# Two small loads move to ScalarE's queue, three more warming products, and one bias product moves behind the first weights of tile 0

## The chip, the cores and the metric

The kernel runs on one core of one Trainium2 chip. Its time is device microseconds (us), the median of several runs; beside them one execution was profiled, and its trace is what the rows below come from. TensorE (PE) does the matrix products, VectorE (DVE) and ScalarE (ACT) the elementwise work, SyncE (SP) issues the transfers (DMAs) between device memory and the on-chip memory; GpSimd (POOL) has almost nothing to do.

## What is computed

An audio tower on 64 x 7 = 448 rows. Patches of 1024 numbers are normalised, scaled by g1 and shifted by b1, multiplied by a 1024 x 512 matrix, given a bias, and normalised again (g2, b2). Then come attention with 16 heads of width 128 and an 8-bit-rounded feed-forward product, both added to the stream. The change touches the first step alone:

```python
def _L0_tok_ref(x, W, b, g1, b1, g2, b2):
    x = x[:, :n_patch * TIN, :].reshape(bsz, n_patch, TIN * F)
    x = layer_norm(x, g1, b1, EPS)
    x = jnp.einsum('bpd,dh->bph', x, W) + b
    return layer_norm(x, g2, b2, EPS)
...
h = _L0_tok_ref(x, L0_tok_W, L0_tok_b, L0_tok_g1, L0_tok_b1, L0_tok_g2, L0_tok_b2)
h = h + _L0_attn_ref(_layernorm(h, axis=-1), L0_attn_W_Q, L0_attn_W_K, L0_attn_W_V, L0_attn_W_O)
h = h + _L0_ffn_ref(_layernorm(h, axis=-1), L0_ffn_weight, L0_ffn_weight_scale, L0_ffn_bias)
```

## The kernel before

The 448 rows are four tiles of 112 rows. Each engine has its own program, written out by hand in order; engines meet only at semaphores, and an engine that waits holds back all that stands behind it in its program.

**SyncE** issues every load, all on one queue. The first are the two halves of patch tile 0 (`x_in`), then, once VectorE has cleared two tiles, the bias row `tok_b`, the identity `ident_sb` for transposes, and the two columns `g1_col` and `b1_col` (the trace calls them g_col and b_col; 128 partitions of 8 numbers, so many tiny pieces). Behind them come the embedding weights `tokw_raw` in four pieces of 512 KB with patch tile 1 between the first and the second, then patch tiles 2 and 3, the rows g2 and b2, the mask, and the heads' weights.

**TensorE** first runs `keep_warm`: WARM_START = 6 small products of a tile of ones with itself, whose result nobody reads. Then it waits for `tok_b` to land and starts the accumulators of tiles 1, 2 and 3 with their bias (`begin_with_bias`, line 342: a product of a tile whose first row is ones with a tile whose first row is the bias, 112 x 512). Then `patch_transposes(0)` (line 336) turns the normalised tile 0 in eight pieces; `begin_with_bias(0)`; and `embed(0)` (line 353) multiplies the eight turned pieces by the eight slices of weights, two slices for each landed piece of weights. A matrix product in full 32-bit precision shows as two records in the trace. Before slice 6 of `embed(0)` stand the transposes of tile 1, before slice 4 of `embed(1)` those of tile 2, and so on; from there on the program goes through the tiles, then through the heads in pairs, then through the feed-forward part.

**ScalarE** takes the square root for tile 0's norm (line 686; its first root loads the table of the function), normalises the second half of tile 0 (line 691), waits for the two columns, and then copies the turned pieces out of PSUM in eight instructions (line 702, `patch_evacuate`), in which it applies g1 and b1. `take_root` waits for all twelve constants `eps_4`.

**VectorE** clears tiles and writes constants, then takes tile 0's mean and variance (lines 949, 951), makes the reciprocal root in four small steps (lines 960 to 983) and normalises the first half of tile 0 (line 1063). For tiles 1 and 2 it does the same up to line 983 and ScalarE normalises the whole tile.

Of the kernel before, what the change touches and what calls it, by code (L numbers as in the profile page):

```python
# [7 lines left out]
ACT = mybir.ActivationFunctionType  # L8
# [7 lines left out]
ROWS = BATCH * PATCHES  # L16
IN_DIM = 1024
D = 512
WARM_START, WARM_STATS, WARM_RSTD, WARM_SCALE = 6, 2, 3, 3
HEADS, E = 16, 128  # L20
PAIRS = HEADS // 2
TILES = 4
KD_ALL, KD_HALF = D // 128, D // 256
TR = ROWS // TILES
KIN = IN_DIM // 128
# [14 lines left out]
ROOTS = {0: LN_EPS, 1: LN_EPS, 2: LN_EPS, 3: LN_EPS, TILES: LN_EPS, 2 * TILES: NORM_EPS, TILES + 1: LN_EPS,  # L40
         2 * TILES + 1: NORM_EPS, TILES + 2: LN_EPS, 2 * TILES + 2: NORM_EPS, TILES + 3: LN_EPS,
         2 * TILES + 3: NORM_EPS}
# [6 lines left out]
def audio_tower(nc, patches, tok_w, heads_w, ffn_w, tok_g1, tok_b1, tok_b, tok_g2, tok_b2,  # L49
# [4 lines left out]
    with ExitStack() as ctx:  # L54
        def sb(name, shape, dt=F32):
            return ctx.enter_context(nc.sbuf_tensor(name, shape, dt))

        def sem(name):
            return ctx.enter_context(nc.semaphore(name))
# [4 lines left out]
        g1_col = sb("g1_col", [128, KIN])  # L64
        b1_col = sb("b1_col", [128, KIN])
# [59 lines left out]
        eps_4 = sb("eps_4", [TR, len(ROOTS)])  # L125
        root = sb("root", [TR, len(ROOTS)])
        last_root = sb("last_root", [TR, TILES])
# [15 lines left out]
        cols_landed = sem("cols_landed")  # L143
# [5 lines left out]
        x_landed = [sem(f"x_landed{t}") for t in range(TILES)]  # L149
# [8 lines left out]
        eps_ok = sem("eps_ok")  # L158
# [72 lines left out]
        def loop_pairs(eng, step):  # L231

            with eng.Fori(0, (PAIRS - 2) // 2) as i:
                step(i * 4 + 2, i * 2 + 1, 1)
                step(i * 4 + 4, i * 2 + 2, 0)
# [5 lines left out]
        @block.sync  # L241
        def _(sp):
            def load(dst, src, landed):
                sp.dma_start(dst, src).then_inc(landed, 16)

            def load_tokw(i):
                a, b = TOKW_PIECES[i]
                load(tokw_raw[:, a:b, :], tok_w[:, a:b, :], tokw_landed[i])

            for c, landed in ((slice(0, 512), x_landed[0]), (slice(512, IN_DIM), x0_rest_landed)):  # L250
                load(x_in[:, 0, c], patches[0][:, c], landed)
            sp.wait_ge(bias_cleared, 2)
            load(tok_b_rows[0:1, :], tok_b[0:1, :], tok_b_landed)
            load(ident_sb[:], ident, ident_landed)
            load(g1_col[:], tok_g1, cols_landed)
            load(b1_col[:], tok_b1, cols_landed)
            load_tokw(0)
            load(x_in[:, 1, :], patches[1], x_landed[1])
            load_tokw(1)
            load_tokw(2)  # L260
            load_tokw(3)
            load(x_in[:, 2, :], patches[2], x_landed[2])
            load(x_in[:, 3, :], patches[3], x_landed[3])
            load(g2_row[:], tok_g2.to_broadcast([TR, D]), rows_landed)
            load(b2_row[:], tok_b2.to_broadcast([TR, D]), rows_landed)
            load(mask_sb[:], mask, late_landed)
            load(ffn_scale_col[:], ffn_scale.to_broadcast([128, 1]), late_landed)
            sp.wait_ge(ffn_b_cleared, 1)
            for row in (0, B_LO):
                load(ffn_b_raw[row:row + 1, :], ffn_bias, late_landed)  # L270
            def load_qkv(h, s):
                sp.dma_start(raw_qkv[s][:], heads_w[h][:, 0:QKV]).then_inc(qkv_landed[s], 16)

            def load_out(h, s):
                sp.dma_start(raw_out[s][:], heads_w[h][:, QKV:WCOLS]).then_inc(out_landed[s], 16)

            for s in range(2):
                load_qkv(s, s)
            for s in range(2):
                load_out(s, s)  # L280
            sp.dma_start(ffnw_raw[:], ffn_w).then_inc(ffnw_landed, 16)
            for s in range(2):
                sp.wait_ge(qkvw_hi_ok, s + 1)
                sp.wait_ge(qkvw_lo_ok, s + 1)
                load_qkv(s + 2, s)

            def load_pair(a, p, g):
                for s in range(2):
                    sp.wait_ge(qkvw_hi_ok, a + (s + 1))
                    sp.wait_ge(qkvw_lo_ok, a + (s + 1))  # L290
                    load_qkv(a + (s + 2), s)
                for s in range(2):
                    sp.wait_ge(outw_hi_ok, a + (s - 1))
                    sp.wait_ge(outw_lo_ok, a + (s - 1))
                    load_out(a + s, s)

            loop_pairs(sp, load_pair)
            for s in range(2):
                sp.wait_ge(outw_hi_ok, HEADS - 3 + s)
                sp.wait_ge(outw_lo_ok, HEADS - 3 + s)  # L300
                load_out(HEADS - 2 + s, s)
            for i, (t, c) in enumerate(RESULTS):
                sp.wait_ge(y_ok, i + 1)
                sp.dma_start(out[t][:, c], h_sb[:, t, c]).then_inc(out_stored, 16)
            sp.wait_ge(out_stored, 16 * len(RESULTS))
# [3 lines left out]
        def _(pe):  # L309
# [14 lines left out]
            def patch_transposes(t):  # L324
                if t == 0:
                    pe.wait_ge(ident_landed, 16)
                    pe.wait_ge(x0_half_normed, 1)
                else:
                    pe.wait_ge(x_normed, t + 1)
                if t >= 2:  # L330
                    pe.wait_ge(xt_ok, KIN * (t - 1))
                for k in range(KIN):
                    if t == 0 and k == KIN // 2:
                        pe.wait_ge(x_normed, 1)
                    b = 2 * (t % 2) + k // 4
                    mm = nc.tensor.transpose(bank[b][:, k % 4 * TR:(k % 4 + 1) * TR],  # L336
                                             x_in[:, t, k * 128:(k + 1) * 128], ident_sb[0:TR, 0:TR])
                    if k % 4 == 3:
                        mm.then_inc(xt_ps, 1)

            def begin_with_bias(t):
                nc.tensor.matmul(acc[t][0:TR, :], first_ones[:], tok_b_rows[:], start=True, stop=False,  # L342
                                 skip_group_check=True)

            def embed(t, ahead_of):
                for k in range(KIN):
                    if k in ahead_of:
                        ahead_of[k]()
                    for i, (first_chunk, _) in enumerate(TOKW_PIECES):
                        if t == 0 and k == first_chunk:  # L350
                            pe.wait_ge(tokw_landed[i], 16)
                    pe.wait_ge(xt_ok, KIN * t + k + 1)
                    last = nc.tensor.matmul(acc[t][0:TR, :], xt[:, t % 2, k * TR:(k + 1) * TR], tokw_raw[:, k, :],  # L353
                                            start=False, stop=(k == KIN - 1), skip_group_check=True)
                last.then_inc(tok_ps, 1)
# [31 lines left out]
            keep_warm(WARM_START, acc[TILES - 1])  # L387
            pe.wait_ge(bias_ones_ok, 1)
            pe.wait_ge(tok_b_landed, 16)
            for t in range(1, TILES):  # L390
                begin_with_bias(t)
            patch_transposes(0)
            begin_with_bias(0)
            embed(0, {KIN - 2: lambda: patch_transposes(1)})
            embed(1, {KIN // 2: lambda: patch_transposes(2)})
            embed(2, {KIN // 2: lambda: patch_transposes(3)})
            stream_transposes(0)
# [280 lines left out]
        def _(act):  # L678
            def hi_part(dst, src):
                return nc.scalar.copy(dst, src)  # L680

            def take_root(c):
                i = list(ROOTS).index(c)
                act.wait_ge(variance_ok, i + 1)
                act.wait_ge(eps_ok, len(ROOTS))
                nc.scalar.activation(root[:, i:i + 1], moments[:, c, 1:2], ACT.Sqrt, bias=eps_4[:, i:i + 1],
                                     scale=4.0).then_inc(root_ok, 1)
# [38 lines left out]
            def split_out(p, s):  # L726
                act.wait_ge(out_landed[s], (p + 1) * 16)
                hi_part(outw_hi[s][:], raw_out[s][:]).then_inc(outw_hi_ok, 1)

            take_root(0)  # L730
            normalise(0, slice(IN_DIM // 2, IN_DIM))
            act.wait_ge(cols_landed, 32)
# [192 lines left out]
        def _(dve):  # L925
# [127 lines left out]
            nc.vector.memset(tok_b_rows[:], 0.0).then_inc(bias_cleared, 1)  # L1053
            dve.wait_ge(bias_cleared, 1)
            nc.vector.memset(first_ones[0:1, :], 1.0).then_inc(bias_ones_ok, 1)
            nc.vector.memset(ffn_b_raw[:], 0.0).then_inc(ffn_b_cleared, 1)
            nc.vector.memset(ones_r[:].bitcast(F32), 1.0).then_inc(ones_ok, 1)
            for i, eps in enumerate(ROOTS.values()):
                nc.vector.memset(eps_4[:, i:i + 1], 4.0 * eps).then_inc(eps_ok, 1)
            patch_moments(0)  # L1060
            need(rsqrt_from_roots([0]))
            negative_mean_scaled(0).then_inc(x_scaled, 1)
# [237 lines left out]
```

## Time and profile before

| | us |
|---|---|
| three runs | 265.77, 266.09, 267.23 (median 266.09) |
| the profiled execution, its own time | 266.61 |
| its span, first to last instruction | 264.8 |
| TensorE busy in the span | 256.3 (97%) |
| share of TensorE in the chain that ended last | 91% |

A span is 1.8 us shorter than the execution's own time. Times in the rows are microseconds from the span's start. SPq rows are the issuing of a transfer, not the transfer. PEld is the loading of stationary data, which overlaps the product before it. The time between two starts is TensorE's pace; a record's own length is longer than that, since products overlap.

### The profile page before, as it was taken

The numbers are of one execution on the slowest core, as the hardware profiler recorded it, in microseconds if no ns is written. First come the engines' busy times: TensorE is split into PE (matmuls) and PEld (weight loads), VectorE is DVE, ScalarE is ACT, GpSimd is POOL, SyncE is SP. The second block draws the span as 40 slices with busy tenths as digits, with TensorE's granted clock in tenths as the row PEclk, the third lists the DMA queues.
The fourth block names the chain that finished last, engine by engine and source line by source line (L and its number), as shares of the span: only waits on it lengthen the run. The fifth ranks groups of instructions, "written<-read, shape, count | busy, mean of one in ns | idle before, by whom it ended". The sixth has DMA issues, their size and how long they took to land.

```text
span 264.8 us, 3840 instructions
## 1 busy us (share of the span) xinstructions
PE 256.3 (97%) x1422; PEld 218.0 (82%) x1422; DVE 157.7 (60%) x321; ACT 124.8 (47%) x216; POOL 0.2 (0%) x4
## 2 busy tenths in 40 slices
PE   7999999999899999999999999999999999999984
PEld 5444447898799999999999999999999999998662
DVE  6257977825828913962493269038723968934884
ACT  2567864444714543533361445425343642536680
POOL 0000000000000000000000000000000000000000
PEclk9999999999999999999999999999999999999999
DMA  5999030141080053032306210630230020000004
GB/s 163 346 272 398 6 119 0 26 155 59 9 308 2 15 186 119 1 110 88 119 0 198 76 43 0 198 119 0 62 136 0 2 79 0 2 0 0 0 4 139
DMA packets 7585, 23.57 MB, mean 89 GB/s; under 512 B 1251, under 2 KB 1715, under 8 KB 7446
## 3 DMA queue, kind: packets, MB, share of 16 engines
q1 hardware_dynamic: 7574, 23.42, 27.2%
q8 instruction: 7, 0.11, 0.2%
q14 instruction: 4, 0.03, 0.0%
HBM read 22.50 MB, written 0.92 MB: 88 GB/s over the span
## 4 chain that ended last, share of the span: by engine, by line
PE 91%; DVE 5%; DMA 1%; issue 1%; ACT 1%; DVEq 0%; ACTq 0%
PE bank L312 14%; PE bank L314 14%; PE bank L313 14%; PE acc L353 10%; PE acc L454 9%; PE bank L429 5%; PE bank L438 5%; PE acc L458 4%; PE acc L648 3%; PE bank L444 3%; PE acc L342 2%; PE bank L421 2%; PE bank L518 2%; PE bank L336 1%; DMA tok_b_rows<-tok_b 1%
## 5 line engine op out<-in xcount | busy, mean ns | idle before, releaser
L312 PE MATMUL bank<-ht_hi,qkvw_hi 128*128 128x448 f32 (+1 forms) x192 | 69.5, 362 | 0.9 <-issue 0.9
L314 PE MATMUL bank<-ht_hi,qkvw_lo 128*128 128x448 f32 (+1 forms) x192 | 69.1, 360 | 0.0
L313 PE MATMUL bank<-ht_lo,qkvw_hi 128*128 128x448 f32 (+1 forms) x192 | 69.1, 360 | 0.0
L942 DVE TENSOR_TENSOR qkvw_lo<-raw_qkv,qkvw_hi 128x1536 fp32r<-128x1536 f32 x16 | 28.1, 1754 | 35.6 <-ACT qkvw_hi L680 35.6
L312 PEld LDWEIGHTS bank<-ht_hi,qkvw_hi 128*128 128x128 f32 x192 | 36.1, 188 | 3.9 <-issue 1.2
L314 PEld LDWEIGHTS bank<-ht_hi,qkvw_lo 128*128 128x128 f32 x192 | 36.1, 188 | 2.8
L313 PEld LDWEIGHTS bank<-ht_lo,qkvw_hi 128*128 128x128 f32 x192 | 36.1, 188 | 2.7
L353 PE MATMUL acc<-tokw_raw,xt 128*112 128x512 f32 x64 | 28.5, 592 | 0.0
L680 ACT CAST qkvw_hi<-raw_qkv 128x1536 fp32r<-128x1536 f32 x16 | 23.5, 1470 | 0.0
L1112 DVE COPY prob_t<-bank 112x448 f32<-112x448 f32 x8 | 5.0, 625 | 29.1 <-PE bank L421 29.1
L353 PEld LDWEIGHTS acc<-tokw_raw,xt 128*112 128x112 f32 x64 | 10.9, 177 | 13.6 <-issue 10.9
L454 PE MATMUL acc<-z_hi,outw_hi 128*128 128x448 f32 x56 | 21.0, 375 | 0.0
L454 PE MATMUL acc<-z_hi,outw_lo 128*128 128x448 f32 x56 | 20.4, 365 | 0.0
L680 ACT CAST z_hi<-bank 128x448 fp32r<-128x448 f32 x16 | 8.5, 534 | 18.1 <-PE bank L429 18.1
L702 ACT ACTIVATE xt<-bank,b_col,g_col 128x112 f32<-128x112 f32 x32 | 11.4, 455 | 5.9 <-PE bank L336 5.9
L458 PE MATMUL acc<-z_lo,outw_hi 128*128 128x448 f32 x56 | 13.6, 365 | 0.0
L680 ACT CAST outw_hi<-raw_out 128x512 fp32r<-128x512 f32 x16 | 9.9, 619 | 5.1 <-PE acc L458 5.1
L1087 DVE SCALAR_TENSOR_TENSOR prob<-bank,mask_sb 112x448 f32<-112x448 f32 x8 | 5.0, 625 | 11.1 <-PE bank L438 11.1
L775 ACT COPY tokw_raw<-bank 128x448 f32<-128x448 f32 x8 | 4.3, 534 | 15.3 <-PE bank L314 15.3
L779 ACT COPY tokw_raw<-bank 128x448 f32<-128x448 f32 x8 | 4.3, 532 | 15.3 <-PE bank L314 15.3
L783 ACT COPY x_in<-bank 112x512 f32<-112x512 f32 x16 | 8.8, 588 | 5.4 <-PE bank L444 5.4
L458 PEld LDWEIGHTS acc<-z_lo,outw_hi 128*128 128x128 f32 x56 | 10.5, 188 | 0.8
(145 smaller groups left out, 392.8 us busy)
## 6 DMA issues: line engine op xcount, KB each, us to landing
raw_qkv<-heads_w SPq DMA_DIRECT2D x16, 768.0 KB, 4.3
raw_out<-heads_w SPq DMA_DIRECT2D x16, 256.0 KB, 4.6
tokw_raw<-tok_w SPq DMA_DIRECT2D x4, 512.0 KB, 7.0
x_in<-patches SPq DMA_DIRECT2D x3, 448.0 KB, 10.0
ffnw_raw<-ffn_w SPq DMA_DIRECT2D x1, 1024.0 KB, 16.0
out<-h_sb SPq DMA_DIRECT2D x3, 224.0 KB, 2.6
x_in<-patches SPq DMA_DIRECT2D x2, 224.0 KB, 2.8
g_row<-tok_g SPq DMA_DIRECT2D x1, 224.0 KB, 11.1
```

The lines of the kernel that those rows point to most:

```text
L312: nc.tensor.matmul(ps, hi, whi, start=first, stop=False, skip_group_check=True)
L313: nc.tensor.matmul(ps, hi, wlo, start=False, stop=False, skip_group_check=True)
L314: return nc.tensor.matmul(ps, lo, whi, start=False, stop=last, skip_group_check=True)
L353: last = nc.tensor.matmul(acc[t][0:TR, :], xt[:, t % 2, k * TR:(k + 1) * TR], tokw_raw[:, k, :], start=False, stop=(k == KIN - 1), skip_gr ...
L429: last = nc.tensor.matmul(bank[b][:, c], v_nat[g][s][:, t, :], prob_t[s][:, c], start=True, stop=True)
L438: last = nc.tensor.matmul(bank[b][0:TR, c], q_t[s][:, c], k_t[s][:, c], start=True, stop=True)
L454: nc.tensor.matmul(acc[c][:, 0:ROWS], w[:, c * 128:(c + 1) * 128], all_rows(z_hi[s]), start=False, stop=False, skip_group_check=True)
L458: last = nc.tensor.matmul(acc[c][:, 0:ROWS], outw_hi[s][:, c * 128:(c + 1) * 128], all_rows(z_lo[s]), start=False, stop=False, skip_group_ ...
L680: return nc.scalar.copy(dst, src)
L702: nc.scalar.activation(xt[:, t % 2, k * TR:(k + 1) * TR], bank[2 * (t % 2) + half][:, k % 4 * TR:(k % 4 + 1) * TR], ACT.Identity, bias=b1_ ...
L783: nc.scalar.copy(v_nat[g][s].rearrange("p t e -> p (t e)"), bank[b][0:TR, :]).then_inc(vn_ok, 1)
L942: return nc.vector.tensor_tensor(dst, src, hi.bitcast(F32), ALU.subtract)
```

## The change

- SyncE no longer loads the two columns. ScalarE issues both on its own queue, after tile 0's first half has landed, and before its first root.
- ScalarE's first instruction becomes a square root of a constant into `last_root`, a tile that is written again before it is read; so the function's table is loaded there.
- On VectorE the twelve constants of `eps_4` move ahead of two other memsets.
- TensorE runs nine warming products instead of six, then two bias products (tiles 1 and 2) instead of three; the third (tile 3) comes before slice 2 of `embed(0)`.

```diff
-WARM_START, WARM_STATS, WARM_RSTD, WARM_SCALE = 6, 2, 3, 3
+WARM_START, WARM_STATS, WARM_RSTD, WARM_SCALE = 9, 2, 3, 3
...
             load(ident_sb[:], ident, ident_landed)
-            load(g1_col[:], tok_g1, cols_landed)
-            load(b1_col[:], tok_b1, cols_landed)
             load_tokw(0)
...
             pe.wait_ge(tok_b_landed, 16)
-            for t in range(1, TILES):
-                begin_with_bias(t)
+            begin_with_bias(1)
+            begin_with_bias(2)
             patch_transposes(0)
             begin_with_bias(0)
-            embed(0, {KIN - 2: lambda: patch_transposes(1)})
+            embed(0, {2: lambda: begin_with_bias(TILES - 1), KIN - 2: lambda: patch_transposes(1)})
...
+            act.wait_ge(eps_ok, 1)
+            nc.scalar.activation(last_root[:, 0:1], eps_4[:, 0:1], ACT.Sqrt)
+            act.wait_ge(x_landed[0], 16)
+            act.dma_start(g1_col[:], tok_g1).then_inc(cols_landed, 16)
+            act.dma_start(b1_col[:], tok_b1).then_inc(cols_landed, 16)
             take_root(0)
...
             nc.vector.memset(first_ones[0:1, :], 1.0).then_inc(bias_ones_ok, 1)
+            for i, eps in enumerate(ROOTS.values()):
+                nc.vector.memset(eps_4[:, i:i + 1], 4.0 * eps).then_inc(eps_ok, 1)
             nc.vector.memset(ffn_b_raw[:], 0.0).then_inc(ffn_b_cleared, 1)
             nc.vector.memset(ones_r[:].bitcast(F32), 1.0).then_inc(ones_ok, 1)
-            for i, eps in enumerate(ROOTS.values()):
-                nc.vector.memset(eps_4[:, i:i + 1], 4.0 * eps).then_inc(eps_ok, 1)
             patch_moments(0)
```

TensorE at the start of its program, before: warming products, bias products (acc<-tok_b_rows,first_ones), transposes (bank<-ident_sb,x_in) and weights (acc<-tokw_raw,xt).

```order
L320 MATMUL acc<-ones_sb 112x112 x6
L342 MATMUL acc<-tok_b_rows,first_ones 112x512 x3
L336 MATMUL bank<-ident_sb,x_in 128x112 x8
L342 MATMUL acc<-tok_b_rows,first_ones 112x512
L353 MATMUL acc<-tokw_raw,xt 112x512 x6
L336 MATMUL bank<-ident_sb,x_in 128x112 x8
```

The same place now (line numbers of the changed kernel are two lower here).

```order
L318 MATMUL acc<-ones_sb 112x112 x9
L340 MATMUL acc<-tok_b_rows,first_ones 112x512 x2
L334 MATMUL bank<-ident_sb,x_in 128x112 x8
L340 MATMUL acc<-tok_b_rows,first_ones 112x512
L351 MATMUL acc<-tokw_raw,xt 112x512 x2
L340 MATMUL acc<-tok_b_rows,first_ones 112x512
L351 MATMUL acc<-tokw_raw,xt 112x512 x4
L334 MATMUL bank<-ident_sb,x_in 128x112 x8
```

Three products were added ahead of the bias, and one bias product went from ahead of the first transposes to between slices 1 and 2 of tile 0's embedding.

ScalarE at the start of its program, before: its table load, tile 0's root and half norm, and the copies that apply g1 and b1.

```order
L686 ACT_TABLE_LOAD
L686 ACTIVATE root<-moments,eps 112x1
L691 ACTIVATE x_in<-x_in,nmr,rstd 112x512
L702 ACTIVATE xt<-bank,b_col,g_col 128x112 x8
L686 ACTIVATE root<-moments,eps 112x1
```

The same place now.

```order
L729 ACT_TABLE_LOAD
L729 ACTIVATE last_root<-eps 112x1
L731 DMA g_col<-tok_g 128x8
L732 DMA b_col<-tok_b 128x8
L684 ACTIVATE root<-moments,eps 112x1
L689 ACTIVATE x_in<-x_in,nmr,rstd 112x512
L700 ACTIVATE xt<-bank,b_col,g_col 128x112 x8
```

One small root and two DMA issues now stand ahead of tile 0's root; the copies that need the two columns stand where they stood.

## Rows read from the trace of the kernel before

**Rows 1.** The page: busy time and the chain that ended last.

```profile
PE 256.3 (97%) x1422; PEld 218.0 (82%) x1422; DVE 157.7 (60%) x321; ACT 124.8 (47%) x216; POOL 0.2 (0%) x4
...
PE 91%; DVE 5%; DMA 1%; issue 1%; ACT 1%; DVEq 0%; ACTq 0%
```

**Rows 2.** Chain that ended last, first 12 us, start us, us, what.

```profile
1.68 2.42 DMA tok_b_rows<-tok_b
4.10 0.14 issue
4.23 5.38 PE acc L342 x6
9.62 0.77 PE bank L336 x8
10.38 0.86 PE acc L342 x2
11.24 0.86 PE acc L353 x2
```

**Rows 3.** Timeline of PE: start us, us, what [idle before, releaser], in narrow windows.

```profile
1.04 2.58 PE L320 MATMUL acc<-ones_sb 112*112 112x112 f32 x12 [1.04 <-DVE ones_sb L1051]
...
3.04 0.58 PE L320 MATMUL acc<-ones_sb 112*112 112x112 f32 x2
...
4.23 1.17 PE L342 MATMUL acc<-tok_b_rows,first_ones 112*112 112x512 f32 x1 [0.61 <-DMA tok_b_rows<-tok_b]
...
7.75 1.86 PE L342 MATMUL acc<-tok_b_rows,first_ones 112*112 112x512 f32 x2
...
8.60 1.01 PE L342 MATMUL acc<-tok_b_rows,first_ones 112*112 112x512 f32 x1
...
9.45 0.93 PE L336 MATMUL bank<-ident_sb,x_in 112*128 112x112 f32 x8
10.22 1.02 PE L342 MATMUL acc<-tok_b_rows,first_ones 112*112 112x512 f32 x2
11.08 1.88 PE L353 MATMUL acc<-tokw_raw,xt 128*112 128x512 f32 x4
```

**Rows 4.** Stretches: length, busy us of each engine, PEclk, DMA share, GB/s.

```profile
2.00:3.00 1.00, 1.00 (x7) 1.00 (x7) 0.64 (x14) 0.20 (x1) 0.00 (x0) 1.00 0.95 346
3.00:4.00 1.00, 0.62 (x4) 0.35 (x2) 0.56 (x1) 1.00 (x1) 0.00 (x0) 1.00 0.60 166
4.00:5.00 1.00, 0.77 (x1) 0.45 (x2) 0.96 (x3) 0.08 (x1) 0.00 (x0) 1.00 0.49 82
...
10.20:41.60 31.40, 31.40 (x100) 14.41 (x98) 22.01 (x72) 23.19 (x52) 0.00 (x0) 1.00 0.62 205
45.00:240.00 195.00, 193.38 (x1172) 181.33 (x1171) 110.73 (x172) 82.95 (x131) 0.00 (x0) 1.00 0.22 72
```

**Rows 5.** Timeline of ACT and DVE at the start, same columns.

```profile
2.79 1.28 ACT L686 ACT_TABLE_LOAD   x1 [2.79 <-DVE eps L1059]
5.07 0.29 ACT L686 ACTIVATE root<-moments,eps 112x1 f32<-112x1 f32 x1 [0.99 <-DVE moments L951]
6.24 0.81 ACT L691 ACTIVATE x_in<-x_in,nmr,rstd 112x512 f32<-112x512 f32 x1 [0.87 <-DVE nmr L983]
10.10 2.80 ACT L702 ACTIVATE xt<-bank,b_col,g_col 128x112 f32<-128x112 f32 x8 [3.05 <-PE bank L336]
...
3.44 1.36 DVE L949 BATCH_NORM_STATS2 stats<-x_in 112x6 f32<-112x512 f32 x2 [0.79 <-DMA x_in<-patches]
6.12 0.54 DVE L1063 TENSOR_SCALAR x_in<-x_in,moments,rstd 112x512 f32<-112x512 f32 x1
```

**Rows 6.** DMA issues (KB each, us to landing); the last line: all four of tokw_raw.

```profile
g_col<-tok_g SPq DMA_DIRECT2D x1, 4.0 KB, 2.0
b_col<-tok_b SPq DMA_DIRECT2D x1, 4.0 KB, 2.0
...
tokw_raw<-tok_w SPq DMA_DIRECT2D x1, 512.0 KB, 4.2
...
tokw_raw<-tok_w SPq DMA_DIRECT2D x1, 512.0 KB, 6.6
...
DMA to landing us min/median/max: 4.2/7.0/8.6
```

**Rows 7.** Timeline of SP, the issuing of the first loads.

```profile
2.42 0.43 SPq L244 DMA_DIRECT2D g_col<-tok_g  x1
2.89 0.43 SPq L244 DMA_DIRECT2D b_col<-tok_b  x1
3.37 0.43 SPq L244 DMA_DIRECT2D tokw_raw<-tok_w  x1
...
4.31 1.42 SPq L244 DMA_DIRECT2D tokw_raw<-tok_w  x3
```

**Rows 8.** Timeline, tile 2's way from its landing to its transposes.

```profile
15.85 1.29 DVE L949 BATCH_NORM_STATS2 stats<-x_in 112x6 f32<-112x512 f32 x2 [1.93 <-DMA x_in<-patches]
17.17 0.21 DVE L951 BATCH_NORM_AGGREGATE moments<-stats 112x2 f32<-112x12 f32 x1
...
18.15 0.30 ACT L686 ACTIVATE root<-moments,eps 112x1 f32<-112x1 f32 x1
18.34 1.46 ACT L702 ACTIVATE xt<-bank,b_col,g_col 128x112 f32<-128x112 f32 x4
...
19.65 1.27 ACT L691 ACTIVATE x_in<-x_in,nmr,rstd 112x1024 f32<-112x1024 f32 x1
...
21.73 0.14 PEld L336 LDWEIGHTS bank<-ident_sb,x_in 112*128 112x128 f32 x1 [0.25 <-issue]
```

## The prediction, made before the changed kernel ran

> **What bounds the kernel now.** I began with the page: TensorE is busy 97% of the span and is 91% of the chain that ended last [rows 1]. So what counts is where TensorE's own unbroken work begins, how fast it goes, and where it waits. The table of stretches says where it waits: from 10.20 to 41.60 it is busy 31.40 of 31.40 us, and in the long part with the heads 193.38 of 195.00 [rows 4]. Nothing there waits for loads. The change can therefore act only before 10.2 us, and what it gains there is passed on whole, if nothing behind becomes late.
>
> The chain of the first 12 us [rows 2] runs: the bias row's load (1.68 to 4.10), then TensorE without a gap: three bias products, eight transposes, one bias product, embedding. The weights that are to "go sooner" are not in it, nor are the two columns.
>
> The timeline of TensorE shows two things more [rows 3]. There is a pause: the warming products' records end at 3.62 and the bias begins 0.61 us later, at 4.23, when its row has landed. And the products are slow at first. The sixth bias record begins at 8.60 and the next work at 9.45, 0.85 us for 512 columns; the fifth begins at 7.75, again 0.85 ahead. After 9.45 the two records of the same product take 0.86 together (10.22 to 11.08), 0.43 each. So up to about 9.45 TensorE went at half pace, the 1.2 GHz level, and then at 2.4. The column of the granted clock says 1.00 in these slices [rows 4] and doesn't show this; the starts do. Before the pace rose, TensorE had worked without a pause since 4.23, for 5.22 us. The 2.6 us of warming ahead of the pause had not sufficed.
>
> **The change, part by part.**
>
> *Three more warming products.* Six take twelve records, which began at 1.04, the last at 3.04 + 0.19 = 3.23 [rows 3], about 0.19 apart. Six records more put the last at 4.36 and TensorE's next start at 4.55. The row of the bias is there at 4.10. So the pause is gone, and the bias begins 0.32 late, at 4.55 instead of 4.23. What matters more is the pace. Unbroken work now begins at 1.04, not 4.23. The trace shows no second rise of the pace from which to say what it needs. I bound it: at one end the pace is up when the bias begins (4.55), at the other it rises where it rose, at 9.45. Between, I take the one case that the trace has: 5.22 us after unbroken work begins, which is 6.26.
>
> With 6.26: from 4.55 the slow pace does 1.71 / 0.855 = 2.0 records of the two bias products' four; the other two take 2 x 0.43 = 0.86. Bias ends at 7.12. The transposes began at 9.45, so they begin 2.33 earlier. They can: the first half of tile 0 is normalised at 6.12 + 0.54 = 6.66, the second at 6.24 + 0.81 = 7.05 [rows 5].
>
> *One bias product moved.* It costs 2 x 0.43 = 0.86 at the fast pace behind slice 1, where it cost 1.71 at the slow one. The work is not gone. Net: 2.33 - 0.86 = **1.47 us sooner** from slice 2 on.
>
> The ends. Fast from 4.55: bias ends at 4.55 + 1.72 = 6.27, but the transposes wait for 6.66 and their second half for 7.05; half of the eight take 0.39, so they end at about 7.55 instead of 10.22: 2.67 - 0.86 = 1.8 sooner. Rise still at 9.45: bias ends at 7.96, the eight transposes at twice 0.77 end at 9.5, tile 0's bias begins 0.7 sooner, and 0.86 goes back: **0.1 to 0.2 later**. So the moved product and the queue change alone bring nothing; the whole gain is the pace.
>
> On this the Trainium skill, "TensorE: Matmul & The Clock Gate", Part 1, says that the point at which the clock rises is run-variable for one and the same kernel, as it depends on how the start falls. The starts of one profiled run can't show that; by that page the profiled pair may differ by more or less than the medians do.
>
> *Two issues off SyncE.* g_col and b_col took from 2.42 to 3.37 [rows 7], so tokw_raw and all behind it are issued 0.95 sooner. The DMA engines were busy 0.60 and 0.49 of the slices 3:4 and 4:5 [rows 4], so there is room, and I expect landings 0.5 to 0.95 sooner. Is that needed? Slice 0 now starts at 7.12 + 0.77 + 0.86 = 8.75; its weights landed at 3.37 + 4.2 = 7.6 already before. Slice 2 starts at 8.75 + 4 x 0.43 + 0.86 = 11.33; its piece landed at 4.31 + 6.6 = 10.9 [rows 6], now near 10. Even unmoved it is in time. Worth nothing by itself: it covers a margin that shrinks from 1.9 us to 0.4.
>
> Tile 2 is the tightest behind. Its load landed at 15.85, its norm was done at 19.65 + 1.27 = 20.92, and TensorE wanted it at 21.73 [rows 8]. TensorE now wants it at 20.26. ScalarE's copies move with TensorE, so the root may be taken once the moments are there, at 17.4 instead of 18.15 even with an unmoved landing; then 0.3 for the root, 1.31 for the other four copies and 1.27 for the norm, 20.3. Just in time; with the load sooner there is 0.5 or more to spare. Zero.
>
> *ScalarE's new head.* The table load (1.28) began at 2.79, when the constants were written; TensorE waits for none of this, since the root waits for the moments at 5.07 [rows 5]. Now it stands ahead of all waits of data. The small root costs about 0.29. After tile 0's landing (3.44, where VectorE began) come two issues; on SyncE such an issue took 0.43, so they end at about 4.35. The root at 5.07 has 0.7 left. If an issue on ScalarE cost 0.8 or more, the root would slip, and behind it the norm of tile 0, which TensorE now wants at 7.12 and gets at 6.66 and 7.05; so 1.1 per issue would still cost only some tenths. The reordered memsets of VectorE keep their sum and end before the 0.79 us that it stands idle [rows 5]. Zero.
>
> *The columns' landing.* ScalarE needs them when the first four transposes are through: 10.10 before, 7.77 now [rows 5]. They are issued at 3.45 and 3.9 and took 2.0 on a quiet queue [rows 6]: 5.9. The other bound is the weights' row in the same traffic, 6.6 from issue to landing: 10.5. I take a value near the first, 6 to 7, since they are 4 KB each and stand first on a queue of their own, while tokw_raw had earlier loads in front of it.
>
> The Trainium skill, "DMA: Bandwidth & Descriptors", "Issuing engines are not separate DMA queues", says that loads issued from several engines run on the same DMA engines, interleave, and that spreading them saves only the sequencer's issue time, usually small beside the transfer. That speaks against a gain from sooner weights, as the sum does here (0.95 us of issue, worth zero).
>
> **The sum.** Span 264.8 - 1.47 = 263.3, own time 266.61 - 1.47 = 265.14. The profiled execution lies 0.52 above the median 266.09; of the four executions shown the mean is 266.43, and with 1.47 less it is 264.96. I predict **265.0**.
>
> **Rivals.**
>
> *A. The pace rises where it did.* For it: the trace has one rise only, and nothing in it ties the rise to the pause. Against it: 2.6 us of products ahead of the pause did not help. 266.4 + 0.15 = 266.6. Chance 0.13.
>
> *B. The columns land late, slower than before.* ScalarE's copies, and behind them slice 0, wait for two small loads that now share the DMA engines with 512 KB pieces. Slice 0 wants its copy at about 8.3, a copy takes 0.45; so it costs from a landing at about 7.85 on, one for one, eats the 1.47 by 9.3, and beyond makes the kernel slower. At 10.5 (6.6 from issue) it is 2.65 - 1.47 = 1.2 slower: 267.6. If they land like the last of the weights (8.6 from issue is the longest of the four [rows 6], so 12.5) it is over 269. Chance 0.07 to be slower than before.
>
> *C. The gain is full, and more is hidden.* Pace up at once: 266.4 - 1.8 = 264.6, and if the unprofiled runs keep to the median, 264.3. Chance 0.2.
>
> *D. The forecast,* 264.6 to 265.5: chance 0.6.
>
> **How the numbers follow.** The runs shown differ by 1.46 us among themselves, as much as the gain. The range takes in the forecast, C, and A up to the part below 266.4: **264.1 to 266.4**. It leaves out most of B and part of A. About 0.5% (1.33 us) is what a measurement of this kernel can tell from no change, and the forecast stands almost on that line: 1.1 against the median shown, 1.47 by the sum. Half of the forecast's chance and most of C go to faster, 0.42; the rest with A to same, 0.51; slower by more than 0.5% is the far part of B, 0.07.
>
> **What would show it.** Right: no idle time before the first bias record; bias records 0.85 apart at first and 0.43 before the transposes begin; transposes at about 7.1; slice 2 near 11.3; the four pieces of tok_w landing at least half a microsecond sooner; TensorE still unbroken to 41. Wrong: all four bias records 0.85 apart (A); ScalarE's first copy released by the load of g_col or b_col instead of by TensorE (B); TensorE idle before slice 2 or before tile 2's transposes, for which I allow nothing.

## The result: 2.5% slower

| | before | changed |
|---|---|---|
| median, 6 runs each, us | 266.53 (265.77 to 267.35) | 273.00 (271.85 to 274.68) |
| ratio, 95% interval | | 1.025 (1.021 to 1.029) |
| profiled execution, own time | 266.61 | 272.63 |
| its span | 264.8 | 270.8 |
| TensorE's share of the chain | 91% | 88% |

The prediction was 265.0 with a range to 266.4; the measured 273.0 lies 6.6 us above the range. Rival B, late columns, to which the text gave 0.07, is what happened, and it cost more than its price there.

The page of the changed kernel names it in the chain that ended last. Beside [rows 1] there is now a load in it, 3% of the span (columns: share of the span by engine, then by line, of which the start stands here):

```profile
PE 88%; DMA 4%; DVE 4%; ACT 1%; issue 1%; ACTq 0%; DVEq 0%
PE bank L310 14%; PE bank L311 14%; PE bank L312 14%; PE acc L351 11%; PE acc L452 9%; PE bank L427 5%; PE bank L436 5%; PE acc L456 4%; DMA b_col<-tok_b 3%; PE acc L646 3%; PE bank L442 3%; PE bank L419 2%; PE bank L516 1%; DMA x_in<-patch
```

The same chain in order of time, changed kernel, first 20 us (start us, us, what), against [rows 2]. A load of 4 KB holds it for 8.84 us:

```profile
3.93 8.84 DMA b_col<-tok_b
12.77 0.03 issue
12.79 0.45 ACT xt L700
13.24 0.14 issue
13.38 3.72 PE acc L351 x4
17.10 1.71 PE acc L340 x2
18.81 3.67 PE acc L351 x8
```

TensorE's timeline of the changed kernel, against [rows 3]:

```profile
1.04 3.70 PE L318 MATMUL acc<-ones_sb 112*112 112x112 f32 x18 [1.04 <-DVE ones_sb L1054]
4.53 2.37 PE L340 MATMUL acc<-tok_b_rows,first_ones 112*112 112x512 f32 x4
6.88 0.96 PE L334 MATMUL bank<-ident_sb,x_in 112*128 112x112 f32 x8
7.67 1.02 PE L340 MATMUL acc<-tok_b_rows,first_ones 112*112 112x512 f32 x2
13.38 3.72 PE L351 MATMUL acc<-tokw_raw,xt 128*112 128x512 f32 x4 [4.68 <-ACT xt L700]
16.90 1.91 PE L340 MATMUL acc<-tok_b_rows,first_ones 112*112 112x512 f32 x2
18.61 1.73 PE L351 MATMUL acc<-tokw_raw,xt 128*112 128x512 f32 x3
```

Up to 8.5 us everything is as forecast and a little better: no pause ahead of the bias, four bias records in 2.35 us, transposes at 6.88 instead of 9.45. Then nothing for 4.68 us. And when work goes on, two slices and a bias product (six records) take from 13.38 to 18.61, 5.23 us, 0.87 each: the slow pace is back. This time the granted clock shows it: it reads 1.00 in the first two of the idle microseconds shown here, 0.50 while the six records run (the 1.2 GHz level), and rises again behind them. Stretches of the changed kernel (length, busy us of PE, PEld, DVE, ACT, POOL, then PEclk, DMA share, GB/s):

```profile
10.00:12.00 2.00, 0.00 (x0) 0.00 (x0) 1.35 (x4) 0.00 (x0) 0.00 (x0) 1.00 1.04 393
12.00:14.00 2.00, 0.62 (x1) 0.45 (x2) 0.00 (x0) 1.21 (x4) 0.00 (x0) 0.58 1.06 285
14.00:16.00 2.00, 2.00 (x3) 0.61 (x2) 0.17 (x2) 1.76 (x6) 0.00 (x0) 0.50 1.03 272
16.00:18.00 2.00, 2.00 (x4) 0.86 (x3) 1.90 (x6) 1.24 (x1) 0.00 (x0) 0.50 1.12 284
18.00:20.00 2.00, 2.00 (x4) 0.72 (x4) 0.19 (x2) 0.00 (x0) 0.00 (x0) 0.71 0.99 304
```

The sum to the start of slice 2. It began at 11.08 + 1.72 = 12.80 before and begins at 18.61 now, 5.81 later:

- slice 0 would have begun at 7.67 + 0.86 = 8.53 instead of 11.08: -2.55;
- the moved bias product at the fast pace: +0.86;
- the wait from 8.53 to 13.38: +4.85;
- six records at the slow pace, 5.23 instead of 2.58: +2.65.

Together 5.81. The first record of slice 2 still took 0.71 instead of 0.43 (it began at 18.61, the next at 19.32), which makes the transposes of tile 1 start 6.09 later (22.32 against 16.23). At the last norm the difference is 5.78, where VectorE begins the chain's last result 6.40, for a reason told in the last section; the spans differ by 6.0.

Why the wait: ScalarE's timeline. Its half norm is done at 7.12, its copies wait until 12.79 for b_col, issued at 3.93. Before, [rows 5], they waited for TensorE.

```profile
3.49 0.39 ACTq L731 DMA_DIRECT2D g_col<-tok_g  x1
3.93 0.44 ACTq L732 DMA_DIRECT2D b_col<-tok_b  x1
...
6.31 0.81 ACT L689 ACTIVATE x_in<-x_in,nmr,rstd 112x512 f32<-112x512 f32 x1 [0.88 <-DVE nmr L986]
12.79 2.79 ACT L700 ACTIVATE xt<-bank,b_col,g_col 128x112 f32<-128x112 f32 x8 [5.67 <-DMA b_col<-tok_b]
```

And why the load took so long: the DMA view of the changed kernel, packets by queue (q1 is SyncE's, q10 ScalarE's; packets, MB, share of 16 engines) in the windows 6:7, 7:8 and 10:11. Until 7 us not one packet of q10 has gone, 3.5 us after its first issue, while q1 has 0.67 to 0.99 of the engines' time in every microsecond from 4 to 7. Its first packets are few, 11 beside 85; by 10 us the queues take turns, 109 packets to 105:

```profile
q1 hardware_dynamic: 81, 0.31, 98.5%
...
q1 hardware_dynamic: 85, 0.30, 111.0%
q10 hardware_dynamic: 11, 0.00, 0.8%
...
q1 hardware_dynamic: 109, 0.39, 98.5%
q10 hardware_dynamic: 105, 0.00, 6.4%
```

The taking of turns is what the Trainium skill says in "DMA: Bandwidth & Descriptors", section "Queues, rings and completion order": each engine goes round its queues at packet granularity. The trace agrees from 9 to 11 us (89 packets to 87, then 109 to 105), and not before: 85 to 11 from 7 to 8, 61 to 40 from 8 to 9, and none from 3.5 to 7.

### The profile page after: what moved, and what is told of

The parts are those of the page before. It is cut to its first block, busy times and chain, and to the rows that moved or that the text cites. A ratio compares the mean times of both kernels' runs of the same rounds, so it can differ in the third digit from the quotient of the medians.

```text
span 270.8 us, 3853 instructions
## 1 busy us (share of the span) xinstructions
PE 259.4 (96%) x1428; PEld 220.9 (82%) x1428; DVE 157.5 (58%) x321; ACT 124.9 (46%) x217; POOL 0.2 (0%) x4
## 4 chain that ended last, share of the span: by engine, by line
PE 88%; DMA 4%; DVE 4%; ACT 1%; issue 1%; ACTq 0%; DVEq 0%
PE bank L310 14%; PE bank L311 14%; PE bank L312 14%; PE acc L351 11%; PE acc L452 9%; PE bank L427 5%; PE bank L436 5%; PE acc L456 4%; DMA b_col<-tok_b 3%; PE acc L646 3%; PE bank L442 3%; PE bank L419 2%; PE bank L516 1%; DMA x_in<-patches 1%; PE bank L334 1%
## 5 line engine op out<-in xcount | busy, mean ns | idle before, releaser
L351 PE MATMUL acc<-tokw_raw,xt 128*112 128x512 f32 x64 | 30.7, 627 | 4.7 <-ACT xt L700 4.7
L351 PEld LDWEIGHTS acc<-tokw_raw,xt 128*112 128x112 f32 x64 | 11.5, 188 | 20.0 <-issue 16.9
```

## The experiments

Each kernel was timed beside the kernel before on the same chip. Four were made from the changed kernel first: one takes the move back, one makes only the move, one makes it earlier, one keeps TensorE at work in the wait.

### e1: the columns on SyncE's queue again

```diff
             load(ident_sb[:], ident, ident_landed)
+            load(g1_col[:], tok_g1, cols_landed)
+            load(b1_col[:], tok_b1, cols_landed)
             load_tokw(0)
...
-            act.wait_ge(x_landed[0], 16)
-            act.dma_start(g1_col[:], tok_g1).then_inc(cols_landed, 16)
-            act.dma_start(b1_col[:], tok_b1).then_inc(cols_landed, 16)
```

> The changed kernel with the two columns issued by SyncE again, ahead of the first weights, and all else as changed (nine warming products, two bias products first, table load at the head). Theory: the whole loss comes from the late columns on ScalarE's queue, and the warming part of the prediction holds. Then the columns land near 4.9 us, slice 0 starts near 8.5 instead of 13.4, and the kernel is 1.4 to 1.7 us faster than before: ratio 0.994 to 0.995, about 264.9. Rival: the nine products and the moved bias product cost something themselves; then the ratio is at or over 1.000.

Measured: 265.34 against 266.59, ratio 0.9954 (0.9935 to 0.9973). The whole loss is gone, and the warming part is worth 1.25 us (the interval reaches from 0.7 to 1.7), near the 1.47 of the sum. But its TensorE timeline isn't the middle case of the forecast. It is the early end that the text had worked out as rival C: the pace is up when the bias begins (four records, 0.43 apart), and the transposes then wait 0.70 for tile 0's half norm. Slice 2 begins at 11.22, 1.58 sooner than before.

```profile
4.40 1.88 PE L342 MATMUL acc<-tok_b_rows,first_ones 112*112 112x512 f32 x4
6.99 0.96 PE L336 MATMUL bank<-ident_sb,x_in 112*128 112x112 f32 x8 [0.70 <-DVE x_in L1065]
7.79 1.02 PE L342 MATMUL acc<-tok_b_rows,first_ones 112*112 112x512 f32 x2
8.64 1.88 PE L353 MATMUL acc<-tokw_raw,xt 128*112 128x512 f32 x4
```

### e2: only the columns moved

The changed kernel with WARM_START = 6, and TensorE's bias products where they were.

```diff
-            begin_with_bias(1)
-            begin_with_bias(2)
+            for t in range(1, TILES):
+                begin_with_bias(t)
...
-            embed(0, {2: lambda: begin_with_bias(TILES - 1), KIN - 2: lambda: patch_transposes(1)})
+            embed(0, {KIN - 2: lambda: patch_transposes(1)})
```

> The kernel before with only the move of the columns to ScalarE's queue (and the table load and memsets that go with it): six warming products and three bias products first, as before. Theory: b_col lands near 12.8 here too, TensorE is through with its bias products at 11.1 and slice 0 starts near 13.4 instead of 11.1, 2.3 us later; TensorE stands idle only some 2.3 us, and if its pace stays up, the kernel is 2.3 us slower: ratio 1.009. If its pace falls too, 2 us more: ratio 1.016. Rival (the loss in the changed kernel is not from this move): ratio 1.000.

Measured: 271.55 against 266.59, ratio 1.018 (1.013 to 1.023). The move alone makes the loss. b_col took 9.74 us, slice 0 began at 14.27 after 3.87 us of idle time, and the twelve records behind it took 7.07 us where before twelve took 5.31: the pace fell here too, and the granted clock reads 0.50 from 16 to 18 us.

```profile
3.92 9.74 DMA b_col<-tok_b
...
14.27 7.07 PE acc L351 x12
```

### e3: the columns first of all

ScalarE issues the columns at 0.73 and 1.18, without the wait for tile 0.

```diff
+            act.dma_start(g1_col[:], tok_g1).then_inc(cols_landed, 16)
+            act.dma_start(b1_col[:], tok_b1).then_inc(cols_landed, 16)
             act.wait_ge(eps_ok, 1)
             nc.scalar.activation(last_root[:, 0:1], eps_4[:, 0:1], ACT.Sqrt)
-            act.wait_ge(x_landed[0], 16)
-            act.dma_start(g1_col[:], tok_g1).then_inc(cols_landed, 16)
-            act.dma_start(b1_col[:], tok_b1).then_inc(cols_landed, 16)
             take_root(0)
```

> The changed kernel, but ScalarE issues the two columns as its first instructions, without waiting for tile 0. Theory (the columns are slow because they meet the weights' large pieces in the DMA engines): at 0.8 us the engines are nearly empty, the columns land by about 4 us, long before 7.8, and the kernel is 1.2 to 1.7 us faster than before; tile 0 may land a few tenths later. Rival (ScalarE's queue is slow in itself, whatever the traffic): they land 8 to 9 us after their issue, near 9.5 to 10, slice 0 starts near 10.3 and the gain is gone: ratio 1.000 or more.

Measured: 266.54 against 266.59, ratio 0.9991 (0.997 to 1.001). Half a hit. The columns landed 3.2 and 3.4 us after their issue, by 4.6, so ScalarE's queue is not slow in itself, and slice 0 began at 8.80. But the gain of e1 is not there. The loads behind landed later: the first weights were issued at 2.43 and landed 5.9 later, at 8.3; in e1 they were issued at 3.37 and landed at 7.7. Tile 2 was issued at 5.38 and landed 11.2 later, at 16.6; in e1, issued at 5.87, at 15.8. The DMA view has the first weights' time to landing in its last column, e3 above, e1 below:

```profile
tokw_raw<-tok_w SPq DMA_DIRECT2D x1, 512.0 KB, 5.9
...
tokw_raw<-tok_w SPq DMA_DIRECT2D x1, 512.0 KB, 4.3
```

So loads issued sooner landed later. In this trace TensorE stood idle only 0.2 us for it, ahead of tile 2's transposes, while the span is 0.9 longer than e1's; the trace accounts for a part of the lost gain. e10 tests whether the early issue is the reason.

### e4: TensorE kept at work in the wait

```diff
             begin_with_bias(0)
+            keep_warm(24, acc[TILES - 1])
             embed(0, {2: lambda: begin_with_bias(TILES - 1), KIN - 2: lambda: patch_transposes(1)})
```

> The changed kernel with 24 more warming products between tile 0's bias product and slice 0, where TensorE stands idle 4.68 us for the columns (24 x 0.19 us = 4.6 us at the fast pace). Theory: 2.65 us of the loss are the slow pace after the idle time; with TensorE kept at work slices 0 and 1 and the third bias product go at 0.43 us a record, not 0.855, and the kernel is 2.5 us faster than the changed one: near 270.3, ratio to before 1.015. Rival (the pace after the wait doesn't hang on idle time, or the loss is all waiting): no change, ratio 1.025.

Measured: 270.82 against 266.59, ratio 1.0136 (1.009 to 1.018), 2.2 us under the changed kernel's 273.00, although b_col took 10.3 us in its trace. The slices after the wait went at 0.45 a record (the third bias product began 1.78 after slice 0, against 3.52 in the changed kernel):

```profile
8.61 4.88 PE L318 MATMUL acc<-ones_sb 112*112 112x112 f32 x48
14.90 1.94 PE L351 MATMUL acc<-tokw_raw,xt 128*112 128x512 f32 x4 [1.42 <-ACT xt L701]
```

So the loss has two parts, waiting and the pace lost by waiting, and the second is about 2 us of it (2.2 between medians of four and six runs).

### e5: one load instead of two

The columns lie side by side in device memory and in one tile `gb_col` of 128 x 16.

```diff
-            act.dma_start(g1_col[:], tok_g1).then_inc(cols_landed, 16)
-            act.dma_start(b1_col[:], tok_b1).then_inc(cols_landed, 16)
+            act.dma_start(gb_col[:], tok_g1).then_inc(cols_landed, 16)
```

> The changed kernel, but both columns lie side by side in device memory and ScalarE loads them with one transfer of 128 pieces of 64 bytes instead of two of 128 pieces of 32 bytes. Theory (each small piece waits for a turn beside a large one, and the count of pieces is the price): in the changed kernel's trace half of the small packets were through by about 10 us; so the load lands near 10.5 instead of 12.8, slice 0 starts near 11.1, TensorE stands idle 2.5 us and the kernel is 0.5 to 1 us slower than before (1.5 more if the pace falls): ratio 1.002 to 1.008. Rival (the delay is a fixed one of a second queue behind the weights, whatever it carries): it lands at 11.2 or later, as g_col did: ratio 1.010 or more.

Measured: 272.03 against 266.06, ratio 1.0235 (1.019 to 1.028). My theory falls: half the packets on ScalarE's queue (144 instead of 288), and it landed no sooner, 9.48 us after its issue:

```profile
3.53 9.48 DMA gb_col<-tok_g
13.01 0.03 issue
13.04 0.45 ACT xt L700
```

The count of small pieces is not the price. What is left is the load beside it.

### e7: the columns on SyncE's queue behind 960 KB

```diff
             load_tokw(0)
             load(x_in[:, 1, :], patches[1], x_landed[1])
+            load(g1_col[:], tok_g1, cols_landed)
+            load(b1_col[:], tok_b1, cols_landed)
             load_tokw(1)
```

(and not issued by ScalarE)

> The changed kernel with the columns on SyncE's queue, but behind the first weights and patch tile 1 (960 KB ahead of them), issued near 3.4 and 3.8, as late as ScalarE issued them. Theory (on one queue pieces go in order and a small load costs little; on a queue of its own each small piece waits its turn): they land right behind tile 1, at 9.5 to 10, three us sooner than from ScalarE's queue; slice 0 starts near 10.3, ratio 1.001 to 1.004. Rival (the traffic at that time is the cause, whichever the queue): they land near 12.5 and the ratio is near 1.025.

Measured: 267.26 against 266.06, ratio 1.005 (1.002 to 1.008). g_col, issued at 3.36, landed at 8.5, b_col, issued at 3.83, at 10.6; slice 0 began at 11.2. I had written 9.5 to 10 for the landing, 10.3 for slice 0 and at most 1.004 for the ratio, so each came out somewhat higher. It is still over 2 us sooner than from ScalarE's queue at nearly the same moment of issue. With large loads in the engines, a place in the same line behind 960 KB was better than the head of a line of its own.

```profile
3.83 6.77 DMA b_col<-tok_b
10.60 0.03 issue
10.63 0.45 ACT xt L702
```

### e11: only one piece of weights ahead

```diff
             load_tokw(0)
+            sp.wait_ge(cols_landed, 32)
             load(x_in[:, 1, :], patches[1], x_landed[1])
```

> The changed kernel, but SyncE holds everything behind the first piece of weights until the columns have landed, so that only 512 KB stand beside them in the DMA engines. Theory (a load on the second queue waits until the large loads handed to the engines before and with it are through): the columns land when the first weights do, at 7 to 8 instead of 12.8; slice 0 starts near 8.7, and slice 2 then waits for its weights, issued some 4 us later than in the changed kernel. Rival (8 to 9 us is what the second queue takes in this stretch, whatever is beside it): they land near 12.5.

Measured in one execution: b_col, issued by ScalarE at 4.00 as in the changed kernel, took 3.39 us, not 8.84. Slice 0 began at 8.70, and slice 2 waited 1.60 for its weights; own time 266.56. The packets of window 5:6 show why: with q1 running dry, 217 of the 288 went in one microsecond.

```profile
q1 hardware_dynamic: 66, 0.21, 54.3%
q10 hardware_dynamic: 217, 0.01, 11.8%
```

So the cause of the late columns is shown to be the large loads handed to the engines behind the first one: with them b_col took 8.8 to 10.3 us in three traces, without them 3.39. What in the engines makes the second queue wait 3.5 us or more for its first turn is not shown. The first weights, with nothing issued behind them, landed at 7.0 here, sooner than in any other trace.

### e8: six warming products

The kernel of e1 with WARM_START back at 6.

```diff
-WARM_START, WARM_STATS, WARM_RSTD, WARM_SCALE = 9, 2, 3, 3
+WARM_START, WARM_STATS, WARM_RSTD, WARM_SCALE = 6, 2, 3, 3
```

> The kernel of e1_cols_on_sync (columns on SyncE) with six warming products instead of nine. Theory of the prediction: the pause ahead of the bias row comes back, TensorE keeps the slow pace through the bias products and the transposes, and the whole gain goes: ratio 0.999 to 1.002. Rival (the gain of e1_cols_on_sync is from the moved bias product or ScalarE's head): ratio 0.995 stays.

Measured: 266.05 against 266.06, ratio 0.9995 (0.997 to 1.002). The gain of e1 goes with the three products. A pause of 0.38 us is back, the four bias records take 3.52 (4.01 to 7.53), and the transposes 1.49 instead of 0.80:

```profile
4.01 3.72 PE L342 MATMUL acc<-tok_b_rows,first_ones 112*112 112x512 f32 x4 [0.38 <-DMA tok_b_rows<-tok_b]
7.53 1.70 PE L336 MATMUL bank<-ident_sb,x_in 112*128 112x112 f32 x8
9.02 1.15 PE L342 MATMUL acc<-tok_b_rows,first_ones 112*112 112x512 f32 x2
```

### e9 and e12: three bias products first; nine warming products alone

e9 is e1 with TensorE's bias products placed as in e2. e12 is the kernel before with WARM_START = 9 and nothing else.

> The kernel of e1_cols_on_sync with nine warming products but three bias products ahead of the transposes, as before. Theory: once the pace is up a bias product costs 0.86 us wherever it stands; but TensorE stood idle 0.70 us ahead of the first transposes for tile 0's norm in that trace, and the third bias product fills this, so the end is 0 to 0.7 us sooner than there: ratio 0.992 to 0.996. Rival (moving it is where the gain comes from): ratio 0.998 or more.

> The kernel before with nine warming products instead of six and nothing else. Theory: the gain is wholly the closed pause ahead of the bias row and the sooner pace; three bias products fill the wait for tile 0's norm, so the ratio is 0.995, as in e9_three_biases, which differs only by ScalarE's early table load and the order of two memsets. Rival (the early table load had a share): 0.997 to 1.000.

Measured: e9 265.09 against 266.06, ratio 0.9956 (0.994 to 0.998); e12 264.70 against 266.15, ratio 0.9941 (0.992 to 0.997). So moving the bias product brings nothing that can be measured, nor does ScalarE's early table load: one changed number in the kernel before carries the whole gain.

The trace of e9 holds a surprise. The head of TensorE's program is that of e1 up to the second bias product, and yet the slow pace lasted into the fourth bias record, and the transposes began at 8.57; slice 2 began 0.88 sooner than before, where in e1 it was 1.58:

```profile
4.53 4.20 PE L342 MATMUL acc<-tok_b_rows,first_ones 112*112 112x512 f32 x6
8.57 0.93 PE L336 MATMUL bank<-ident_sb,x_in 112*128 112x112 f32 x8
```

### e10: columns first, weights held until tile 0 is there

The kernel of e3 with one wait on SyncE.

```diff
+            sp.wait_ge(x_landed[0], 16)
             load_tokw(0)
             load(x_in[:, 1, :], patches[1], x_landed[1])
```

> The kernel of e3_cols_first_of_all, but SyncE waits for the first half of tile 0 before it issues the first weights (near 3.5 instead of 2.43). Theory (in that trace the loads behind landed 0.4 to 0.7 us later than in e1_cols_on_sync although they were issued 0.94 sooner, and TensorE waited for tile 2; early issuing is what cost it the gain): the loads land at the times of e1_cols_on_sync, tile 2 near 15.8, and the ratio falls from 0.999 to 0.995. Rival (issuing the columns from ScalarE is itself the cost, or the difference is not from the loads): the ratio stays at 0.999.

Measured: 264.63 against 266.15, ratio 0.9934 (0.991 to 0.996). The first weights were issued at 3.60 and landed 4.2 later, at 7.8; tile 2 landed at 15.8. Holding the weights 1.2 us made them land 0.5 sooner than in e3 and gave the gain back. It is the fastest median here, but its interval overlaps those of e12, e1 and e9. One thing stays open: in e12's profiled execution the loads landed late as well (5.3 for the first weights, with the issue order of e1), slice 2 waited 0.41 us for its weights, and that was the slowest of its runs, 266.18 against a median of 264.70. So late landings come now and then without early issuing too; with it they showed in each of the six traces that have it and the loads behind (the changed kernel, e2, e3, e4, e5 and e7: first weights at 7.9 to 9.5), and without it in one of six.

## Why the prediction was wrong, step by step

- **What bounds the kernel, the pause, the slow pace:** right. With the pause closed, the pace rose in the changed kernel before the transposes; they began at 6.88 (7.12 in the sum). e8 shows it turned round.
- **The moment of the rise, 6.26, taken as 5.22 us after unbroken work begins:** not borne out as a fixed time. In all ten traces with nine warming products TensorE's work begins at 1.04 or 1.03. The starts put the rise near 4.3 to 4.4 in e1, e5 and e11, between 5.4 and 6.1 in the changed kernel, e3, e4, e10 and e12, and between 7.1 and 7.7 in e7 and e9. With six it came between 7.5 and 8.2 in e2, after 9.0 in e8 and near 9.45 before. So the closed pause brings the rise forward, but 6.26 was one value within a spread of 3 us, and that the changed kernel's trace came near it is luck. What decides it from trace to trace is not shown.
- **The 1.47 us:** right in mechanism, and in size within the noise. e1 measured 1.25, e12 1.45; the single traces gained between 0.88 (e9) and 1.58 (e1) by the start of slice 2. The prediction's remark that one profiled pair can differ from the medians was to the point.
- **The bias product moved, ScalarE's head, the memsets: zero.** Right (e9, e12). An issue on ScalarE took 0.39 to 0.44, the root began at 5.14 instead of 5.07.
- **Landings 0.5 to 0.95 sooner:** wrong. The first weights were issued at 2.42 and took 5.5 us, landing at 7.9; before, 3.37 + 4.2 = 7.6 [rows 6, 7]. Tile 1 landed at 9.7 instead of 9.8, the last weights at 14.5 instead of 13.9. From the engines' share of 0.49 to 0.60 between 3 and 5 us [rows 4] the text concluded that there was room. They did move more there (199 GB/s against 82 from 4 to 5), but no load landed more than 0.1 sooner. That the first weights landed at 7.0 with nothing issued behind them (e11) says that the loads behind are what slows them. It cost nothing in the changed kernel, where all waited for the columns; by e10 it cost e3 its gain.
- **The columns' landing, the step that failed:** "I take a value near the first, 6 to 7, since they are 4 KB each and stand first on a queue of their own". They landed at 11.2 and 12.8, after 7.7 and 8.84 us. Both reasons were beside the point: 4 KB took as long as 512 KB beside it (5.5 to 10.2), half the packets changed nothing (e5), and the place at the head of an own queue was worse than one behind 960 KB (e7). The only rows for a 4 KB load were those of a nearly empty queue [rows 6]; the rows of loads in the same stretch (4.2 to 8.6 from issue) were the nearer ones in what decided, the traffic. They would have given 8 to 12.5 for a need at 7.85.
- **Rival B's price:** it counted the wait one for one and left out that a TensorE which stands idle loses its pace. [rows 3] had just shown what idle time ahead of products costs, and the sum of the gain was built on it; the price of the loss was not. The wait was 4.85, the pace 2.65 more up to slice 2 and 0.28 in the record behind it.

## What to carry to other kernels

A small load that somebody waits for belongs ahead of the large ones, whichever queue issues it (e1 from SyncE's, e10 from ScalarE's); on another queue, issued while the DMA engines are full, it can take longer than behind the large loads themselves (e7). Before gaining by fewer issues on one queue, check that the loads behind are limited by their issue at all; here, issued up to 0.95 sooner, none landed more than 0.1 sooner. And when TensorE is made to wait, price the wait and the slow pace after it; where the wait can't be avoided, filler products can recover the second part (about 2 us in e4).

## What the runs showed of the hardware

- Four kilobytes took 1.9 to 2.4 us on SyncE's queue ahead of the weights, 5.1 and 6.8 there behind 960 KB, 3.1 to 3.4 on ScalarE's queue beside tile 0, 2.7 and 3.4 beside one piece of weights, and beside a full row of them 7.7 to 8.0 for the first column and 8.8 to 10.3 for the second.
- The four pieces of weights, issued some 0.95 us sooner, landed 0.5 to 0.95 later (e3 against e1).
- The slow pace came back after TensorE had stood idle 3.87 to 4.80 us (the changed kernel, e2, e5), and not after 1.42 to 1.78 us (e4, e7, e11).
- In the changed kernel's first 9 us the granted clock reads 1.00 in every microsecond, although the bias records begin 0.86 apart at first. Only the starts show the slow pace there.
- TensorE's pace fell near the end too, in the traces of the changed kernel, e3, e10 and e12, and not in those of the others, though that part of the program is the same. In the changed kernel six warming products there took 1.18 us where before they took 0.77, and the path there lost some 0.6 us. The stretch of the changed kernel that shows it, in the columns of [rows 4]:

```profile
256.00:259.00 3.00, 2.87 (x19) 2.69 (x17) 2.27 (x8) 1.63 (x5) 0.00 (x0) 0.65 0.00 0
```

  What decides whether it falls there was not tried. The kernel before has it too, by its runs' mean clock: of the 15 beside e10, five with 0.994 took 266.77 to 267.71 us, ten with 1.000 took 265.16 to 266.37.
